# Which 32 partitions of adj each of the two DMA queues loads

## The reference, cut to what matters

```
h2   = tanh(x @ W_proj + b_proj)
x1   = norm(x + relu(keep350(tanh(adj * adj)) @ (h2 @ W_gcn) + b_gcn))
pos  = (adj > 0) @ x1;   neg = (adj < 0) @ x1
y    = [pos, neg] @ node_w + node_b * diag(adj) + (adj @ x1) @ edge_w + edge_b * diag(adj)
out  = norm(x1 + y)
```

## Time and profile before

| | |
|---|---|
| Median of 3 runs | 657.14 us (654.3 to 657.41) |
| The profiled execution | 656.15 us |
| Its span, first to last instruction | 653.9 us |
| Granted TensorE clock, mean | 0.981 of full speed |
| PE, DVE, ACT, POOL busy | 615.0, 492.2, 449.1, 122.3 us |
| DMA | 130.62 MB, 200 GB/s over the span |

### The profile page before, as it was taken

The page is one execution under the profiler, slowest core; times in us unless marked ns, Lnnn a source line. Parts: engine busy times, 40 slices in busy tenths (PEclk is TensorE's granted clock), DMA queues, the critical chain, the costliest instruction groups (busy, mean ns, idle before and its releaser), DMA issues.

```text
span 653.9 us, 6778 instructions
## 1 busy us (share of the span) xinstructions
PE 615.0 (94%) x2016; PEld 348.3 (53%) x2016; DVE 492.2 (75%) x689; ACT 449.1 (69%) x302; POOL 122.3 (19%) x71
## 2 busy tenths in 40 slices
PE   6599599999999999999999999999999999999994
PEld 3454244444444444476655555555555555556993
DVE  2462797979797797995758978779688687786845
ACT  2295769797878879641688878787675858676740
POOL 0242446454454535400000000000000000000000
PEclk9699799999999999999999999999999999999997
DMA  9999999999999994000099888788675867765000
GB/s 210 335 209 245 243 331 321 267 305 258 295 257 311 259 286 130 1 1 0 25 254 238 256 248 232 240 220 249 189 212 161 240 198 203 203 181 145 1 17 18
DMA packets 140313, 130.62 MB, mean 200 GB/s; under 512 B 8579, under 2 KB 140294, under 8 KB 140294
## 3 DMA queue, kind: packets, MB, share of 16 engines
q1 hardware_dynamic: 72118, 65.23, 38.1%
q10 hardware_dynamic: 68176, 65.15, 36.0%
HBM read 128.27 MB, written 2.10 MB: 199 GB/s over the span
## 4 chain that ended last, share of the span: by engine, by line
PE 61%; issue 16%; POOL 13%; DVE 5%; ACT 2%; ACTq 2%; DMA 1%; POOLq 0%; SPq 0%; DVEq 0%
PE acc L950 29%; POOL a_cols L305 13%; PE acc L952 8%; PE acc L951 8%; DVE a_cols L495 3%; PE acc L892 3%; PE stage L914 2%; PE stage L970 2%; PE acc L970 2%; ACTq L380 2%; PE stage L843 1%; PE stage L836 1%; DMA early<-in_x_dram 1%; ACT a_cols L424 1%; DVE root L550 1%
## 5 line engine op out<-in xcount | busy, mean ns | idle before, releaser
L495 DVE STREAM_TRANSPOSE a_cols<-a_rows 128x2048 f32<-128x2048 f32 x128 | 293.1, 2302 | 88.8 <-PE acc L952 43.3
L892 PE MATMUL acc<-a_cols,rhs 128*128 128x512 f32 x512 | 224.9, 597 | 7.3 <-ACT a_cols L424 7.3
L950 PE MATMUL acc<-a_cols,rhs 128*128 128x512 f32 x448 | 229.0, 592 | 0.0
L951 PE MATMUL acc<-masks,pos_hi 128*128 128x512 f32 x224 | 178.5, 797 | 0.0
L448 ACT ACTIVATE a_rows<-a_rows 128x4096 f32<-128x4096 f32 x32 | 116.0, 3624 | 74.8 <-DVE a_cols L495 58.4
L892 PEld LDWEIGHTS acc<-a_cols,rhs 128*128 128x128 f32 x512 | 96.7, 192 | 123.9 <-issue 115.7
L305 POOL TENSOR_TENSOR a_cols<-a_cols 128x1024 f32<-128x1024 f32 x64 | 121.5, 1898 | 154.4 <-DVE a_cols L495 154.4
L424 ACT ACTIVATE a_cols<-a_cols 128x2048 f32<-128x2048 f32 x64 | 122.3, 1911 | 17.4 <-POOL a_cols L305 15.8
L451 ACT ACTIVATE a_rows<-a_rows 128x4096 f32<-128x4096 f32 x32 | 116.0, 3624 | 2.9
L950 PEld LDWEIGHTS acc<-a_cols,rhs 128*128 128x128 f32 x448 | 83.9, 189 | 19.3
L420 ACT ACTIVATE a_cols<-a_cols 128x1024 f32<-128x1024 f32 x64 | 67.1, 1049 | 35.4 <-DVE a_cols L495 18.5
(11 more groups left out here) (83 smaller groups left out, 326.4 us busy)
## 6 DMA issues: line engine op xcount, KB each, us to landing
a_rows<-in_adj_dram SPq DMA_DIRECT2D x120, 512.0 KB, 8.2
a_rows<-in_adj_dram ACTq DMA_DIRECT2D x120, 512.0 KB, 8.5
early<-in_x_dram SPq DMA_DIRECT2D x8, 256.0 KB, 6.3
out_dram<-n_rows ACTq DMA_DIRECT2D x7, 256.0 KB, 8.5
out_dram<-n_rows ACTq DMA_DIRECT2D x2, 128.0 KB, 1.8
w_pne<-n_L_gnn_node_weight_dram SPq DMA_DIRECT2D x1, 128.0 KB
w_pg<-in_L_gnn_W_proj_dram ACTq DMA_DIRECT2D x1, 64.0 KB, 2.7
w_pg<-in_L_gnn_W_gcn_dram ACTq DMA_DIRECT2D x1, 64.0 KB, 3.3
```

The source lines that it names most:

```text
L495: nc.vector.transpose(half_out(hs), half_in(s, h % HALVES)).then_inc(turned[layer], 1)
L892: last = nc.tensor.matmul(acc[parity][:], rhs[:, b, :], a_cols[:, h % HSLOTS, k, :], start=(b == 0), stop=(b == BLOCKS - 1))
L950: nc.tensor.matmul(acc[parity][:], rhs[:, b, :], cols, start=(b == 0), stop=False)
L951: nc.tensor.matmul(acc[parity][:], pos_hi[:, b, :], mask, start=False, stop=False)
```

## The change

SP and ACT still issue two quarters each of every piece, at the same places and with the same counts. Only which ones is different: SP had quarters 0 and 1 (partitions 0 to 63) and ACT 2 and 3 (64 to 127); after the change SP has 0 and 2 (0 to 31, then 64 to 95) and ACT has 1 and 3 (32 to 63, then 96 to 127). Nothing else of the program changes.

```
-    SP_QUARTERS = range(QUARTERS // 2)
-    ACT_QUARTERS = range(QUARTERS // 2, QUARTERS)
+    SP_QUARTERS = range(0, QUARTERS, 2)
+    ACT_QUARTERS = range(1, QUARTERS, 2)
```

## The result

| | before | after |
|---|---|---|
| median of 4 runs | 657.2 us (654.3 to 657.4) | 698.0 us (688.5 to 708.5) |
| ratio | 1 | 1.049, 95% interval 1.044 to 1.054 |
| span of the profiled execution | 653.9 us | 706.2 us |
| mean granted clock | 0.981 | 0.957 |

The change makes the kernel slower, by 5 to 8%. Six executions after took 688.5, 688.9, 699.1, 707.1, 708.5 and 709.8 us; the median is of four of them, the ratio compares the lowest two with the kernel before, and the profile is of the one of 708.5. Experiments 5 and 10 ask what stands behind the spread. Both kernels have the same number of instructions, and DVE, ACT and POOL are busy for the same time within 1.3 us. PE is busy for 630.4 us in place of 615.0, at a lower mean clock. So the loss is in the main waiting.

A forecast was written before the change was run, and what follows sets the result against it. PE was taken to pace layer 0, its loads needing 279 GB/s. Start 6.9 plus chunks 2 to 7 19.8 less cover 3 gave +23.7 us on 656.15, so 680 us; range 656 to 706.

The forecast's parts named there:

- The mechanism: Layer 0's loads need 279 GB/s; queues on one half of the partitions move 199, on different halves 346.
- f: Share of bytes the queues move while on different halves; taken as 0.49 for layer 0's chunks 2 to 7.
- 5.27 - 2.24f: Time in us of one step, each queue moving one quarter: 5.27 in conflict, 3.03 on different halves.
- The start: Chunk 0 of layer 0: SP's 5.5 remaining quarters each 1.25 us slower, uncovered, +6.9 us.
- The upper bound: Highest cost of the start, +9.4 us, if the two quarters of chunk 1's first piece are slowed too.
- The chunks of layer 0: Chunks 2 to 7, 48 steps of 4.17 us in place of 3.76: +19.8 us.
- cover: Lead of layer 0's loads before chunk 2 that hides slower steps: 3 us taken off, bounds 0 and 7.
- Layer 1: Asks for 196 GB/s; cost nothing, as 4.5 us of cover at chunk 1's first piece outweighs +3.1.
- Rival 1: The halves do not matter, two queues move 346 GB/s whatever they write: 656 to 657 us, chance 0.12.
- Rival 2: Only the start costs, f staying above 0.67 in layer 0: 663 us, chance 0.14.
- Rival 3: Queues in step, f near 0.1, layer 0 steps of 5.05 us: 722 us, chance 0.09.
- Rival 4: Faster: SP's lone alternating queue reaches both halves at the start, 3.7 us less: 652.5 us, chance 0.05.

The follow-up runs named there:

- experiment 5: The changed kernel run again without edit, six executions: 707.2 us (678.8 to 710.9), the profiled one 678.8.
- experiment 10: The changed kernel run again without edit, a single execution at another time: 709.7 us.
- experiment 1: A separate kernel of loads alone, eight stages varying queues, halves written and columns read: 347 GB/s on different halves, 201 to 212 on the same; no kernel time given.
- experiment 2: The changed kernel with ACT's quarters reversed (3, 1), so the queues alternate on opposite halves: 706.8 us, ratio 1.078 to the kernel before.
- experiment 3: The kernel before with the changed quarters in layer 0's chunk 0 alone: 664.4 us, ratio 1.012.
- experiment 4: The kernel before with the changed quarters in chunks 1 to 7 of layer 0 alone: 698.8 us, against 655.8 for the kernel before.
- experiment 6: The changed kernel with SP on quarters 0 and 3, ACT on 1 and 2, same order of halves: 703.5 us, ratio 1.072.
- experiment 8: The changed kernel with the diagonal's load moved behind layer 0's loads: 691.6 us, 44 us above the same edit on the kernel before.
- experiment 9: The kernel before with the changed quarters in layer 1's loads alone: 657.3 us against 655.5, ratio 1.004.
- the mirror: Another name for experiment 2, the changed kernel with ACT's quarters reversed: 706.8 us.

## Why the prediction was right, and where its sizes were off

**The mechanism held.** The halves set the rate (experiment 1), which the prediction took from one window of 9 us with SP's queue alone; the number of queues and the columns read do not. Layer 0 needs 279 and gets 223; layer 1 needs 196 and hardly notices. The lag is kept while the queues are full (0.08 to 0.10 here, 0.59 and 0.59 in experiment 5). A good lag led to a worse one in the one execution that had it (experiment 2). The blocked issue of ACT was there too: 4.43 us in one issue, 62.9 us of waits behind issues.

Two things in it did not hold. The lag of the totals does not give f by the line 5.27 - 2.24f (below). And chunk 1 was not SP's queue alone at 199 as before: from 67 to 76 us the changed kernel moved 230, of which ACT's queue, late by then as well, had 0.59 of 2.07 MB.

**The start** was to cost 6.9 us, 9.4 at most, and cost 13.0. SP's blocked issue begins at 34.42 in place of 29.58, +4.8: that is the term I had, a little smaller. But the issue itself is held for 26.14 us in place of 21.41, +4.7: the diagonal ahead of it takes longer. I put that down to the slower transfers of ACT's queue that share the engines with it, which no run separates. And from its end to the transposable piece are 18.4 us in place of 14.95 (65.94 less 50.99), +3.5: two queues are on chunk 1 and alternate. The upper bound had the first and the last and left out the middle one. Experiment 3, where only chunk 0 is changed, shows +5.8 at the same mark, about the first term; experiment 4, where chunk 0 is as before, transposes the piece at 69.21, +3.3, about the last. The term also varies from one execution to the next: +5.6 in experiment 5, +14.6 in experiment 10.

**The chunks of layer 0** were to cost 19.8 less 3 of cover, and cost 38.0. This is the mis-sized term, and two things in it were off. The first is the value of f. I took 0.49, the middle of those that last, while the profiled executions of the changed kernel had lags of 0.10, 0.19 and 0.59, and experiments 4 and 6 0.02 and 0.36: mostly below the middle, and three of them below the 0.30 that I had as the lowest of a new start. The second is the line from f to the rate, when f is read off the lag of the totals. Read from the executions above, with 8 steps to a chunk (4 pieces of two steps each). In experiments 4 and 8 SP is ahead by the lag, in the others behind. The last column is the time from the first to the last report of a piece, explained below:

| execution | lag | chunk us | step us | by 5.27 - 2.24f | reports us |
|---|---|---|---|---|---|
| experiment 4 | 0.02 | 37.8 | 4.7 | 5.23 | 11.3 |
| changed kernel | 0.10 | 37.3 | 4.7 | 5.05 | 13.4 |
| experiment 10 | 0.19 | 37.3 | 4.7 | 4.84 | 13.5 |
| experiment 6 | 0.36 | 37.3 | 4.7 | 4.46 | 12.1 |
| experiment 8 | 0.5 | 36.3 | 4.5 | 4.15 | 12.7 |
| experiment 5 | 0.59 | 33.2 | 4.15 | 3.95 | 11.3 |

The rate is almost flat up to a lag of about a third, better than the line where the queues are in step, and worse from there on. The two rates at the line's ends stand by themselves (201 to 212 and 347 in experiment 1). But two alternating queues in the kernel do not reach them: they moved 222 to 225 in step, and 282 for queues in step on opposite halves (experiment 2). A step of 4.67 in place of 3.76, times 48, is +43.7. The 38.0 measured is 5.7 less, which I take for the cover, though no run separates it; I had 3.

The trace shows that a lag of the totals says little of the halves. Each load reports its end in 16 parts, so a piece of four loads in 64 reports, and the trace keeps the time of each. In chunks 2 to 7 of layer 0 the last report comes 5.1 us (median) behind the first in the kernel before, but 11.3 to 13.5 us in the executions of the table and 19.0 in experiment 2. With all parts together it would be about one step, 4.7 us or less. So even at a lag of 0.02 the parts are more than a quarter apart, and some write one half while others write the other. That this is what makes the curve flat is argued and not shown: no run here set the spread by itself.

**Layer 1** was to cost nothing and cost 1.3 in the profile and 1.8 to 2.6 in experiment 9. Of the 1.3, 1.0 come in its first chunk (404.74 less 338.76 against 352.67 less 287.69): that fits a cover of 4.5 us at chunk 1 that is just used up, which no run separates.

**The rivals.** Rival 1 is refuted by experiment 1. Rival 2 (start only, 663) is what experiment 3 makes by hand, 664; none of the three profiled executions of the full change had a lag above 0.67. Rival 3 (in step) had the place that came true, a lag of 0.1, but a step of 5.05 us, which was 4.67; so it gave 722 where 708.5 was measured. Rival 4 falls with the 219 GB/s of the lone, alternating queue.

So the forecast was right in sign, place and cause. Its 680 lies at the low end of what the changed kernel shows (678.8 to 710.9); the median of 698.0 is inside its range of 656 to 706, the profiled 708.5 outside. One execution came out as forecast, that of experiment 5: +5.6 us for the start (6.9), +16.4 for the rest of layer 0 (16.8), a step of 4.15 us (4.17). That is in part luck, since it had a lag of 0.59, for which the line gives 3.95.

What stays open: what in the first 100 us decides the lag of an execution, what spreads the parts of a load, and whether the lag or something that goes with it sets the rate in a changed kernel; no run set the lag by itself.

## What to carry to other kernels

Give each queue a half of the partitions of its own when loads are narrower than 128 partitions: 347 GB/s against 201 to 212, with the DMA share full at both (1.10 and 1.13). Where that separation is left to the timing of two queues, the time of the same program varies (678.8 to 710.9 us here), and a good phase can be lost when a queue runs short (experiment 2). And look at what stands in a queue ahead of the first transfer that someone waits for: moving one load of 4096 single elements gave 1.1% here.

## What the runs showed of the hardware that was not expected

- Two full queues kept their lag to 0.02 quarters over 150 us (experiments 5 and 10, and the changed kernel), and each execution had another one; in experiment 8 it went from 0.7 at 100 us to 0.5 at 250. The times of one program on one core went with it: the profiled executions at 0.59, 0.10 and 0.19 took 678.8, 708.5 and 709.7 us.
- The 16 parts of a load drift apart when the queues alternate between the halves: the 64 reports of a piece span 11.3 to 13.5 us (medians) where they span 5.1 with fixed halves, and 19.0 in the mirror.
- Two alternating queues in step on opposite halves moved 282 GB/s in the kernel for 15 us, where fixed halves moved 345.
- A queue that alternates between the halves has 219 GB/s, hardly more than one that stays on a half (204), while a load over all 128 partitions has 351 on the same queue.
- Two queues in step on the same half moved 222 to 225 GB/s in the kernel and 201 to 212 with the loads alone. In step is meant by their totals, and the spread of the parts goes with it; it is not shown to be the reason.
